# Mixture of experts in a gated block: the second bias as products of 12 rows, the residual put in first

## The chip, the cores and the metric

The kernel runs on one core of one Trainium2 chip. The metric is device time in microseconds (us) for one launch. TensorE (PE in the profile) multiplies matrices, VectorE (DVE) and GpSimd (POOL) do elementwise work, ScalarE (ACT) evaluates functions, SyncE (SP) only issues transfers here. Each engine runs its own instructions in order; semaphores order the engines among each other.

## The reference

Input `x` has 4 batches of 256 tokens with 256 features. The block adds a gated cross attention, then a gated transformer layer: `out = x1 + tanh(g_ffn) * ffn(x1)`. The layer is a layer norm, attention with 16 heads of 128, a residual, a second layer norm and a mixture of four experts. Only this last part is touched:

```
raw  = softmax(x @ w_gate)                      # [tokens, 4]
top_vals, top_idx = top_k(raw, 2)
comb = softmax(top_vals) scattered to [tokens, 4]
hmid = gelu(x @ we1[e] + be1[e])                # per expert e, 256 wide
eout = hmid @ we2[e] + be2[e]
moe  = sum over e of comb[:, e] * eout[:, e]
```

So the second bias contributes `comb @ be2`, a product over four experts. All is computed in f32 accuracy; products of f32 are made from a high part, rounded to the format that TensorE takes in one pass (F32R), and the low rest.

## The kernel before

The 1024 tokens stand as eight tiles of 128 partitions (`NT`), two per batch. `yacc` holds the running output of the second layer, `x_sb` the block's residual. Attention loops over eight pairs of heads with four batches each and takes most of the span; its last output projections end near 400 us, and then the experts follow. Tokens are handled in two halves `c` of 512, experts `e` in each: `m = 4c + e`, eight steps. Order on each engine is written out by hand.

**TensorE.** `middle(n)` makes 128 hidden features for 512 tokens (six products of 512 columns: high by low, low by high, high by high, two slices). There are 16, alternating between banks 0 and 1, and `middle(n)` waits until gelu `n - 2` has left its bank. `expert_out(m)` is 24 products of 256 columns into two banks (6 and 7, or 2 and 3), one for each batch `hf`; it waits for the low parts of the hidden features (`c_gL`) and from `m = 2` on for VectorE's accumulation of `m - 2`. The gate's logits are made transposed, in four strips of 32 partitions of bank 5, then turned by two transposes after `expert_out(0)`. After `expert_out(1)` come `middle(4)` to `middle(7)`, then an `expert_out` after every second `middle`.

**ScalarE** takes gelu out of the bank into `G` and writes its high part to `GH` (L834, L839). Ahead of gelu 4 it evaluates the two exponentials of the gates (L827, L829), each waiting for VectorE. Functions need a table; loading one is an instruction of its own.

**GpSimd** makes the low parts: `GL = G - GH` (L579), and for the normed hidden state (L575).

**VectorE** copies the logits from PSUM (L1190), waits for the turn, copies the gates (L1192), finds the softmax, the two largest and their weights (L1194 to L1227) in a `gate` tile of 128x32, and then does for each step `m`, with `yacc` as an input and an output:

```
ins = dve.scalar_tensor_tensor(yacc[:, n, :], be2_rows[:, e, :], gate[:, 4 * n + e:4 * n + e + 1], yacc[:, n, :], ...)   # L1240, bias
ins = dve.scalar_tensor_tensor(yacc[:, n, :], out_bank(m, hf)[:, 256 * t:256 * (t + 1)], gate[...], yacc[:, n, :], ...)  # L1249
```

four tiles each, so 32 of either kind. `be2_rows` is the bias spread over all 128 partitions by a single broadcast transfer (L318). After the last expert of a half, `yacc * tanh(g_ffn) + x_sb` follows for each batch (L1256, `small[:, 97]` is the gate of the block), and SP writes that batch out (L321). `link` on an engine makes the next instruction wait for the one before.

Of the kernel before, what the change touches and what calls it, by code (L numbers as in the profile page):

```python
# [8 lines left out]
F32R = mybir.dt.float32r  # L9
# [3 lines left out]
ALU = mybir.AluOpType  # L13
ACT = mybir.ActivationFunctionType
AX = mybir.AxisListType

P = 128
B, S, D = 4, 256, 256
# [12 lines left out]
NU = NP * U  # L31
LEAD = 6

E, I, IT = 4, 256, 2
NE = E * IT
# [13 lines left out]
def build_kernel(nc, x, ctx_in, cst, cols, rows, bv, wqkv, wo, w_out_t, w_gate, be2, we, out):  # L49
    with ExitStack() as stack:  # L50
# [10 lines left out]
        x_sb = sb("x_sb", [P, NT, D])  # L61
# [10 lines left out]
        yacc = sb("yacc", [P, NT, D])  # L72
# [4 lines left out]
        small = sb("small", [P, 160])  # L77

        stg = sb("stg", [P, 3, KT, 256])
# [5 lines left out]
        wvH = sb("wvH", [P, KT, 256], F32R)  # L85
        wvL = sb("wvL", [P, KT, 256], F32R)
# [35 lines left out]
        be2_rows = stg[:, 0:2, :, :].rearrange("p w k n -> p (w k n)").rearrange("p (e n) -> p e n", e=E)  # L122

        nh = sb("nh", [P, 2, D])
        qn = sb("qn", [P, 2, 2, D])
# [26 lines left out]
        bank = [ps(f"bank{n}") for n in range(8)]  # L152
# [5 lines left out]
        ident = cst_sb[:, C_ID:C_ID + P]  # L158
# [10 lines left out]
        c_nh c_tr c_hT c_hH c_h gate_zero d_be c_logit c_lgT c_lg_pe c_be c_mid c_gelu c_gH c_gL c_exp_pe c_acc c_fin"""  # L169
        s = {n: sem(n) for n in names.split()}  # L170

        def wait(eng, name, value):
# [100 lines left out]
        def _(sp):  # L273
# [44 lines left out]
            sp.dma_start(be2_rows, be2.rearrange("(o e) n -> o e n", o=1).to_broadcast([P, E, D])).then_inc(s["d_be"], 16)  # L318
            for b in range(B):
                sp.wait_ge(s["c_fin"], b + 1)  # L320
# [270 lines left out]
        def _(act):  # L591
# [103 lines left out]
            for p in range(NPX + VLAG):  # L695
                b, k = divmod(p, XP)
# [146 lines left out]
        def _(dve):  # L843
            seq = [0]

            def link(ins):

                seq[0] += 1
                ins.then_inc(s["dve_seq"], 1)
                dve.wait_ge(s["dve_seq"], seq[0])  # L850
# [65 lines left out]
            q = qn[:, 0, 0, 0:P].rearrange("p (h d) -> p h d", d=XD)  # L916
# [271 lines left out]
            V3 = lambda a: gate[:, a:a + 32].rearrange("p (t e) -> p t e", e=E)  # L1188
            dve.wait_ge(s["c_logit"], 1)
            dve.tensor_copy(nh[:, 0, :], bank[5][:, 0:256]).then_inc(s["c_lgT"], 1)  # L1190
            dve.wait_ge(s["c_lg_pe"], 1)
            link(dve.tensor_copy(Gt(0, 32).rearrange("p (b t e) -> p t b e", t=2, e=E),  # L1192
                                 bank[4][:, 0:256].rearrange("p (t b w) -> p t b w", t=2, b=B)[:, :, :, 0:E]))
# [34 lines left out]
            dve.wait_ge(s["d_be"], 16)  # L1228
            dve.wait_ge(s["b_yadd"], NU // 2)

            for m in range(2 * E):

                c, e = divmod(m, E)
                for hf in range(2):
                    b = 2 * c + hf
                    if m:
                        dve.wait_ge(s["c_acc"], 2 * (m - 1) + hf + 1)
                    for t in range(2):
                        n = 2 * b + t
                        ins = dve.scalar_tensor_tensor(yacc[:, n, :], be2_rows[:, e, :], gate[:, 4 * n + e:4 * n + e + 1], yacc[:, n, :],  # L1240
                                                       ALU.mult, ALU.add)
                    ins.then_inc(s["c_be"], 1)
                for hf in range(2):
                    b = 2 * c + hf
                    dve.wait_ge(s["c_exp_pe"], 2 * m + hf + 1)
                    dve.wait_ge(s["c_be"], 2 * m + hf + 1)
# [5 lines left out]
                    if e == E - 1:  # L1252
                        dve.wait_ge(s["c_acc"], 2 * m + hf + 1)
                        y = yacc[:, 2 * b:2 * b + 2, :].rearrange("p t n -> p (t n)")
                        xb = x_sb[:, 2 * b:2 * b + 2, :].rearrange("p t n -> p (t n)")
                        dve.scalar_tensor_tensor(y, y, small[:, 97:98], xb, ALU.mult, ALU.add).then_inc(s["c_fin"], 1)  # L1256


        @block.tensor
        def _(pe):  # L1260
# [291 lines left out]
            def middle(n):  # L1552
                if n >= 2:
                    pe.wait_ge(s["c_gelu"], n - 1)
                if n == NE:
                    pe.wait_ge(s["c_h"], B)
                middle_part(n, 0, 512).then_inc(s["c_mid"], 1)

            def expert_out(m):
# [4 lines left out]
                for hf in range(2):  # L1564
# [5 lines left out]
                                    [((GH[:, m % 2, k, cut], GL[:, m % 2, k, cut]), (we2H[:, 2 * e + k, :], we2L[:, 2 * e + k, :])) for k in range(IT)])  # L1570
                    ins.then_inc(s["c_exp_pe"], 1)

            pe.wait_ge(s["we_ready"], NP)
            for b in range(2):
                pe.wait_ge(s["c_h"], b + 1)
# [104 lines left out]
```

## Time and profile before

| | |
|---|---|
| time, three runs | 469.63 us median (467.46 to 471.44) |
| the profiled execution | 466.32 us, of it the span of instructions 464.2 |
| busy, share of the span | TensorE 411.2 us (89%), VectorE 370.1 (80%), GpSimd 297.6 (64%), ScalarE 286.5 (62%) |
| instructions | TensorE 3135 products, VectorE 1144, ScalarE 650, GpSimd 429 |
| granted TensorE clock, mean | 0.990 |

All stretches below are in us from the start of the span. A busy share is an average over stages with different limits; what a change in one stage is worth is read from that stage, by what ends its waits last. The chain of waits is followed back from the last instruction: at each step to what released it, or to the instruction before it on its engine. The clock is a share of full speed (2.4 GHz).

### The profile page before, as it was taken

Reading aid. Unit: us, or ns where it says so; the run is one execution under the profiler, and the core shown is the slowest. Engines: PE = TensorE matmul, PEld = TensorE weight load, DVE = VectorE, ACT = ScalarE, POOL = GpSimd, SP = SyncE. Lnnn points to the kernel's source line nnn. Section 1 sums busy time; section 2 is a strip of 40 time slices with the busy share of each in tenths; the row PEclk is TensorE's granted clock in tenths of the full one; section 3 lists DMA queues with packets and bytes.
Section 4 is the critical chain, followed back from the end, with each engine's and each line's share of the span. In section 5 each row is a group of like instructions: output and inputs, shape, how many; then the busy total and the mean of one; then the engine's idle time right before and its main releaser. Section 6 shows DMA issues by size and latency. Waiting matters only on the chain.

```text
span 464.2 us, 10317 instructions
## 1 busy us (share of the span) xinstructions
PE 411.2 (89%) x3135; PEld 357.7 (77%) x3150; DVE 370.1 (80%) x1144; ACT 286.5 (62%) x650; POOL 297.6 (64%) x429
## 2 busy tenths in 40 slices
PE   0477997998898899999999999999999995688994
PEld 0356876886786799899899898998998984577994
DVE  3855568677789988798788888898887868968997
ACT  3357674765235778677677677677677688174440
POOL 5898969720598597486687687677677534163551
PEclk9999999999999999999999999999999999979999
DMA  5600000200255885865865855975855654000011
GB/s 148 195 3 2 1 1 4 92 3 1 47 114 120 180 150 119 193 144 108 195 141 116 189 127 116 203 133 112 215 119 116 146 83 99 7 1 1 1 45 46
DMA packets 71795, 44.53 MB, mean 96 GB/s; under 512 B 57424, under 2 KB 60112, under 8 KB 71760
## 3 DMA queue, kind: packets, MB, share of 16 engines
q1 hardware_dynamic: 67680, 35.42, 36.0%
q10 hardware_dynamic: 4080, 8.69, 6.8%
q8 instruction: 17, 0.28, 0.2%
q14 instruction: 18, 0.15, 0.1%
HBM read 13.68 MB, written 1.05 MB: 32 GB/s over the span
## 4 chain that ended last, share of the span: by engine, by line
PE 67%; DVE 18%; issue 5%; ACT 3%; POOL 3%; DMA 2%; ACTq 0%; SPq 0%; DVEq 0%; POOLq 0%
PE bank L1395 35%; PE bank L1463 5%; PE bank L1510 5%; DVE yacc L1240 3%; PE bank L1462 3%; PE bank L1511 3%; DVE yacc L1249 2%; PE bank L1335 2%; PE bank L1376 2%; POOL room L511 2%; PE bank L1290 2%; PE bank L1311 2%; PE bank L1336 1%; PE bank L1357 1%; DMA qk_room<-qk_room 1%
## 5 line engine op out<-in xcount | busy, mean ns | idle before, releaser
L772 ACT ACTIVATE probs<-sm,nm 128x128 f32<-128x128 f32 (+1 forms) x128 | 57.2, 449 | 43.0 <-DVE nm L1126 43.0
L764 ACT ACTIVATE probs<-turned 128x768 uint16<-128x768 uint16 x64 | 69.1, 1080 | 19.3 <-DMA turned<-halves 18.0
L1395 PE MATMUL bank<-hH,qk_parts 128*128 128x512 f32 x240 | 75.4, 395 | 0.0
L524 POOL COPY halves<-probs 128x768 uint16<-128x768 uint16 x64 | 52.7, 824 | 35.0 <-DVE probs L1172 35.0
L511 POOL TENSOR_TENSOR room<-room,qk_room 128x512 f32<-128x512 f32 x32 | 41.2, 1289 | 33.7 <-DMA qk_room<-qk_room 28.7
L1395 PE MATMUL bank<-hL,qk_parts 128*128 128x512 f32 x120 | 57.7, 481 | 0.9 <-DVE room L1043 0.9
L1395 PEld LDWEIGHTS bank<-hH,qk_parts 128*128 128x128 f32 x240 | 45.2, 188 | 9.5
L1043 DVE SCALAR_TENSOR_TENSOR room<-bank,qk_bias,cst_sb 128x512 f32<-128x512 f32 x64 | 47.5, 742 | 0.0
L1395 PE MATMUL bank<-woL,o_parts 128*128 128x256 f32 x128 | 38.7, 302 | 9.8 <-DVE o_parts L1114 4.0
L1014 DVE TENSOR_REDUCE nxm<-bank 128x2 bf16<-128x512 f32 (+1 forms) x48 | 32.8, 688 | 18.0 <-PE bank L1336 17.4
L1395 PE MATMUL bank<-woH,o_parts 128*128 128x256 f32 x256 | 46.9, 281 | 0.0
L511 POOL TENSOR_TENSOR room<-room,q_room 128x512 f32<-128x512 f32 x32 | 41.2, 1289 | 6.2 <-DMA q_room<-q_room 6.1
L656 ACT ACTIVATE probs<-bank 128x512 f32<-128x512 f32 x48 | 28.4, 596 | 24.9 <-PE bank L1352 14.0
L781 ACT ACTIVATE o_parts<-bank,bv_pair 128x256 fp32r<-128x256 f32 x64 | 30.0, 468 | 16.9 <-PE bank L1511 10.2
L1395 PEld LDWEIGHTS bank<-woH,o_parts 128*128 128x128 f32 x256 | 39.4, 189 | 0.0
L1395 PE MATMUL bank<-wvL,hH 128*128 128x256 f32 x128 | 38.7, 302 | 0.7 <-ACT V L732 0.7
L1510 PE MATMUL bank<-probs,V 128*128 128x256 f32 x128 | 38.2, 379 | 0.2 <-ACT probs L764 0.2
L1463 PE MATMUL bank<-room 128*128 128x256 f32 x128 | 38.2, 380 | 0.0
L579 POOL TENSOR_TENSOR qk_parts<-G,o_parts 128x512 fp32r<-128x512 f32 x16 | 21.7, 1369 | 23.5 <-ACT o_parts L839 23.2
L1395 PE MATMUL bank<-wvH,hH 128*128 128x256 f32 x128 | 36.1, 282 | 0.0
L1395 PE MATMUL bank<-wvH,hL 128*128 128x256 f32 x128 | 36.0, 282 | 0.0
L1043 DVE SCALAR_TENSOR_TENSOR qk_room<-bank,qk_bias,cst_sb 128x512 f32<-128x512 f32 x32 | 24.0, 749 | 14.7 <-PE bank L1395 14.4
(233 smaller groups left out, 1269.0 us busy)
## 6 DMA issues: line engine op xcount, KB each, us to landing
qk_room<-qk_room SPq DMA_DIRECT2D x64, 128.0 KB, 2.4
q_room<-q_room SPq DMA_DIRECT2D x64, 128.0 KB, 2.4
stg<-in_wqkv ACTq DMA_DIRECT2D x6, 768.0 KB, 5.8
stge<-in_we ACTq DMA_DIRECT2D x7, 256.0 KB, 3.1
stg<-in_wqkv SPq DMA_DIRECT2D x2, 768.0 KB, 4.9
stgo<-in_wo ACTq DMA_DIRECT2D x6, 256.0 KB, 3.5
x_sb<-in_x SPq DMA_DIRECT2D x4, 256.0 KB, 4.2
turned<-halves SPq DMA_TRANSPOSE x64, 2.8
```

The lines of the kernel that those rows point to most:

```text
L511: pool.tensor_tensor(v, v, qk_sw[q], ALU.subtract).then_inc(s["rope_done"], 1)
L524: pool.tensor_copy(halves[:, j % 2, :, :], PR[:, j % 2, 0:384].bitcast(U16).rearrange("p (n h) -> p h n", h=2)).then_inc(s["b_split"], 1)
L579: pool.tensor_tensor(GL[:, (n // 2) % 2, n % 2, :], G[:, n % 2, :], GH[:, (n // 2) % 2, n % 2, :].bitcast(F32), ALU.subtract).then_inc(s[" ...
L656: act.activation(prob_slot(m, z), PT_B[p % 2][:, :], ACT.Exp).then_inc(s["s_exp"], 1)
L764: act.activation(PTs[:, 1 - q, 0:384].bitcast(U16).rearrange("p (n h) -> p h n", h=2), turned[:, (j - 3) % 4, :, :].rearrange("p (h c) n - ...
L772: ins = act.activation(PR[:, q, a:e], sm[:, q, a:e], ACT.Exp, bias=nm[:, q, t:t + 1], scale=-1.0, accum_out=rs[:, q, t:t + 1])
L781: act.activation(oH[:, ((j - 4) // 2) % 2, q, :], value_bank(j)[:, 0:256], ACT.Identity, bias=head_bias(j)).then_inc(s["b_oH"], 1)
L1014: dve.tensor_reduce(nxm[:, m % 3, a:a + len(heads)], S_B[p % 2][:, :].rearrange("p (h n) -> p h n", h=len(heads)), AX.X, ALU.max, negate=T ...
L1043: return dve.scalar_tensor_tensor(out.rearrange("p (b t) -> p b t", b=2), source[:, :].rearrange("p (b t) -> p b t", b=2), qk_bias[:, c:c ...
L1395: ins = pe.matmul(outp, l, r, start=(m == 0), stop=(m == n - 1))
L1463: pe.matmul(S_B[j % 2][:, P:3 * P], QT[:, 2 * r, second], QT[:, 2 * r + 1, both], start=True, stop=True).then_inc(s["b_s"], 1)
L1510: pe.matmul(value_bank(j)[:, 0:256], V[:, 2 * b, r * HD:(r + 1) * HD], PTs[:, q, 0:256], start=True, stop=False)
```

## The change

- The bias becomes a product on TensorE. `gates` is split in a high and a low part and packed on 12 columns of a strip of 32 (high, low, high), turned by two transposes (`pack_turn`) and copied to `gates_turned`; `be2_parts` holds, on the same 12 rows of each strip, the bias's high, high and low part. One product over 12 rows then gives `gates @ be2` to the precision of three products. `second_bias(c)` makes four such products of 256 columns for a half, into banks 4 and 5; VectorE adds them with two additions of 128x512.
- The 12 rows come by twelve transfers of 4 rows in place of the broadcast; VectorE splits them, between the copy of the logits and that of the gates.
- The residual is put in ahead: `yacc * tanh(g_ffn) + x_sb` is done before the experts (batches 0 and 1 ahead of the gates, 2 and 3 after expert 1), and the weights of the gates are multiplied by `tanh(g_ffn)`.
- The two-way softmax of the top values is `0.5 +- 0.5 tanh`, with ScalarE's Tanh moved from ahead of gelu 4 to ahead of gelu 5.

```diff
+            for q in range(4):
+                for r in range(3):
+                    row = 32 * q + E * r
+                    sp.dma_start(be2_raw[row:row + E, :], be2).then_inc(s["d_be"], 16)
...
                 if n == 4:
                     act.wait_ge(s["c_gmax"], 1)
                     act.activation(gate[:, 64:96], gate[:, 32:64], ACT.Exp).then_inc(s["c_gexp"], 1)
+                if n == 5:
                     act.wait_ge(s["c_gdiff"], 1)
-                    act.activation(gate[:, 400:408], gate[:, 392:400], ACT.Exp).then_inc(s["c_gexp"], 1)
+                    act.activation(gate[:, 400:408], gate[:, 392:400], ACT.Tanh, scale=-0.5).then_inc(s["c_gexp"], 1)
...
             dve.tensor_copy(nh[:, 0, :], bank[5][:, 0:256]).then_inc(s["c_lgT"], 1)
+            dve.wait_ge(s["d_be"], 16 * 12)
...
+            dve.tensor_scalar(half_g, small[:, 97:98], 0.5, None, ALU.mult)
+            dve.tensor_scalar(minus_half_g, small[:, 97:98], -0.5, None, ALU.mult)
+            dve.tensor_reduce(is_high, by_quad[:, :, 0:2 * E], AX.XY, ALU.add)
+            dve.tensor_reduce(is_low, by_quad[:, :, 2 * E:3 * E], AX.XY, ALU.add)
+            link(dve.tensor_copy(be2_high.bitcast(F32R), be2_raw))
+            link(dve.tensor_tensor(be2_low, be2_raw, be2_high, ALU.subtract))
+            link(dve.tensor_scalar(be2_low, be2_low, is_low, None, ALU.mult))
+            dve.scalar_tensor_tensor(be2_parts, be2_high, is_high, be2_low, ALU.mult, ALU.add).then_inc(s["c_half"], 1)
...
+            residual_form(0)
+            residual_form(1)
             dve.wait_ge(s["c_lg_pe"], 1)
...
-            link(dve.tensor_scalar(Gt(248, 8), Gt(400, 8), 1.0, None, ALU.add))
-            link(dve.reciprocal(Gt(256, 8), Gt(248, 8)))
-            link(dve.tensor_tensor(Gt(264, 8), Gt(256, 8), Gt(400, 8), ALU.mult))
+            dve.tensor_scalar(Gt(256, 8), Gt(400, 8), half_g, half_g, ALU.mult, ALU.add)
+            link(dve.tensor_scalar(Gt(264, 8), Gt(400, 8), minus_half_g, half_g, ALU.mult, ALU.add))
...
+            link(dve.tensor_copy(packed[:, :, :, 0:E].bitcast(F32R), gates))
+            dve.tensor_copy(packed[:, :, :, 2 * E:3 * E], packed[:, :, :, 0:E])
+            dve.tensor_tensor(packed[:, :, :, E:2 * E].bitcast(F32R), gates, packed[:, :, :, 0:E], ALU.subtract).then_inc(s["c_pack"], 1)
...
-                        ins = dve.scalar_tensor_tensor(yacc[:, n, :], be2_rows[:, e, :], gate[:, 4 * n + e:4 * n + e + 1], yacc[:, n, :],
-                                                       ALU.mult, ALU.add)
...
+            accumulate(0)
+            dve.wait_ge(s["c_pack_pe"], 1)
+            dve.tensor_copy(gates_turned, bank[4][:, 0:256]).then_inc(s["c_gT"], 1)
+            add_biases(0)
+            accumulate(1)
+            residual_form(2)
+            residual_form(3)
+            accumulate(2)
+            accumulate(3)
+            accumulate(4)
+            add_biases(1)
+            for m in range(5, 2 * E):
+                accumulate(m)
...
+            def second_bias(c):
...
+                for hf in range(2):
+                    rows_ = slice(32 * (2 * c + hf), 32 * (2 * c + hf) + 3 * E)
+                    for t in range(2):
+                        ins = pe.matmul(bank[4 + hf][:, 256 * t:256 * (t + 1)], gates_turned[rows_, t * P:(t + 1) * P], be2_parts[rows_, :],
+                                        start=True, stop=True)
...
             middle(5)
+            pack_turn()
             middle(6)
-            for n in range(7, 2 * NE):
+            middle(7)
+            second_bias(0)
+            expert_out(2)
+            for n in range(8, 2 * NE):
                 middle(n)
+                if n == 11:
+                    second_bias(1)
                 if n % 2:
                     expert_out((n - 3) // 2)
```

`pack_turn` waits for `c_pack` and makes the two transposes into bank 4. `accumulate(m)` is the four accumulations of L1249; `add_biases(c)` waits for `second_bias(c)` and adds banks 4 and 5 to `yacc`; `accumulate(1)` and `accumulate(5)` wait for it.

## Rows read from the trace of the kernel before

**Rows 1.** Busy by stretch: from:to, us; PE, PEld, DVE, ACT, POOL; clock, DMA, GB/s.

```profile
424.45:425.81 1.36, 0.00 (x1) 0.00 (x1) 1.29 (x6) 1.32 (x3) 0.00 (x0) 1.00 0.00 0
425.81:457.83 32.02, 31.73 (x204) 28.27 (x204) 31.95 (x60) 14.98 (x23) 16.59 (x12) 1.00 0.05 17
```

**Rows 2.** End of the chain of waits: start, us, what.

```profile
460.90 0.75 DVE yacc L1256
```

**Rows 3.** TensorE in order of time: start, us, engine, line, operation [idle before, releaser].

```profile
425.81 0.51 PE L1395 MATMUL bank<-hL,weH 128*128 128x512 f32 x1 [1.36 <-ACT G L834]
...
429.12 0.39 PE L1395 MATMUL bank<-weL,o_parts 128*128 128x256 f32 x1 [0.24 <-POOL qk_parts L579]
...
432.05 0.39 PE L1395 MATMUL bank<-hL,weH 128*128 128x512 f32 x1
...
457.55 0.28 PE L1395 MATMUL bank<-weH,o_parts 128*128 128x256 f32 x1
```

**Rows 4.** VectorE on `yacc`, experts: count; ns min/median/max, first and last start.

```profile
L1240 DVE SCALAR_TENSOR_TENSOR yacc<-stg,gate,yacc x32: 470/474/1522, 425.0 to 458.0; 128x256 f32<-128x256 f32 x32
L1249 DVE SCALAR_TENSOR_TENSOR yacc<-bank,gate,yacc x32: 469/473/480, 426.6 to 460.4; 128x256 f32<-128x256 f32 x32
L1256 DVE SCALAR_TENSOR_TENSOR yacc<-yacc,small,x_sb x4: 752/819/1765, 440.8 to 460.9; 128x512 f32<-128x512 f32 x4
```

**Rows 5.** VectorE and GpSimd side by side; last row: ns min/median/max in attention.

```profile
429.27 3.34 DVE L1240 SCALAR_TENSOR_TENSOR yacc<-stg,gate,yacc 128x256 f32<-128x256 f32 x3
...
429.35 2.98 POOL L579 TENSOR_TENSOR qk_parts<-G,o_parts 128x512 fp32r<-128x512 f32 x2 [0.28 <-ACT o_parts L839]
...
L1171 DVE TENSOR_SCALAR probs<-probs,rs x64: 285/287/1437, 136.4 to 389.0; 128x128 f32<-128x128 f32 x64
```

**Rows 6.** VectorE and GpSimd around the logit copy, in order of time.

```profile
415.31 2.55 POOL L579 TENSOR_TENSOR qk_parts<-G,o_parts 128x512 fp32r<-128x512 f32 x2
417.81 1.29 POOL L575 TENSOR_TENSOR hL<-qk_room,hH 128x512 fp32r<-128x512 f32 x1
...
415.65 0.42 DVE L1190 COPY nh<-bank 128x256 f32<-128x256 f32 x1 [1.43 <-PE bank L1589]
418.86 0.19 DVE L1192 COPY gate<-bank 128x32 f32<-128x32 f32 x1 [2.79 <-PE bank L1595]
```

**Rows 7.** ScalarE at the gates, in order of time.

```profile
416.51 1.28 ACT L827 ACT_TABLE_LOAD   x1
419.53 0.23 ACT L827 ACTIVATE gate<-gate 128x32 f32<-128x32 f32 x1 [1.73 <-DVE gate L1195]
...
425.07 0.69 ACT L834 ACTIVATE G<-bank,cols_sb 128x512 f32<-128x512 f32 x1
425.79 0.63 ACT L839 ACTIVATE o_parts<-G 128x512 fp32r<-128x512 f32 x1
```

**Rows 8.** VectorE's gate arithmetic, two of its steps.

```profile
422.70 0.19 DVE L1216 TENSOR_TENSOR gate<-gate 128x32 f32<-128x32 f32 x1
...
423.34 0.17 DVE L1220 TENSOR_TENSOR gate<-gate 128x8 f32<-128x8 f32 x1
```

**Rows 9.** Turn of the gates, return from 32-column products, issue of the bias transfer.

```profile
L1595 PE MATMUL bank<-cst_sb,nh x2: 270/270/271, 418.4 to 418.6; 128*128 128x128 f32 x2
...
415.51 0.19 PEld L1395 LDWEIGHTS bank<-weL,o_parts 128*128 128x128 f32 x1 [0.41 <-issue]
...
391.74 0.53 SPq L318 DMA_DIRECT2D stg<-in_be  x1
```

**Rows 10.** ScalarE's Tanh at the front.

```profile
18.84 0.20 ACT L694 ACTIVATE small<-rows_sb 128x2 f32<-128x2 f32 x1 [0.26 <-DMA rows_sb<-in_rows]
```

**Rows 11.** Busy time by stretch around the clock's fall; columns as in Rows 1.

```profile
392.96:395.49 2.53, 0.00 (x2) 0.03 (x1) 2.46 (x9) 1.37 (x2) 0.00 (x0) 1.00 0.60 198
400.64:403.35 2.71, 0.00 (x1) 0.01 (x1) 2.57 (x9) 0.00 (x0) 1.18 (x1) 1.00 0.00 0
...
404.03:410.86 6.83, 5.64 (x26) 5.05 (x26) 6.33 (x27) 2.61 (x4) 1.27 (x1) 0.50 0.00 0
```

More of the change, by code:

```diff
@@ L121, in build_kernel @@
         gate = sb("gate", [P, 512])
-        be2_rows = stg[:, 0:2, :, :].rearrange("p w k n -> p (w k n)").rearrange("p (e n) -> p e n", e=E)
+        be2_raw, be2_high, be2_low, be2_parts = stg[:, 0, 0, :], stg[:, 0, 1, :], stg[:, 1, 0, :], wvH[:, 0, :]
+        gates_turned = wvL[:, 0, :]
         nh = sb("nh", [P, 2, D])
@@ L168, in build_kernel @@
         b_s b_max b_exp b_norm b_split d_pt0 d_pt1 b_merge b_pv b_oH b_oL b_wo b_yadd v_pe v_ready
-        c_nh c_tr c_hT c_hH c_h gate_zero d_be c_logit c_lgT c_lg_pe c_be c_mid c_gelu c_gH c_gL c_exp_pe c_acc c_fin"""
+        c_nh c_tr c_hT c_hH c_h gate_zero d_be c_logit c_lgT c_lg_pe c_half c_pack c_pack_pe c_gT c_be c_badd c_res c_mid c_gelu c_gH c_gL c_exp_pe c_acc"""
         s = {n: sem(n) for n in names.split()}
@@ L1190, in _, with residual_form @@
             dve.tensor_copy(nh[:, 0, :], bank[5][:, 0:256]).then_inc(s["c_lgT"], 1)
+            dve.wait_ge(s["d_be"], 16 * 12)
+            is_low, is_high = small[:, 142:143], small[:, 143:144]
+            by_quad = ident.rearrange("p (q w) -> p q w", q=4)
+            half_g, minus_half_g = small[:, 140:141], small[:, 141:142]
+            dve.tensor_scalar(half_g, small[:, 97:98], 0.5, None, ALU.mult)
[6 more added lines that the diff above has]
+            dve.scalar_tensor_tensor(be2_parts, be2_high, is_high, be2_low, ALU.mult, ALU.add).then_inc(s["c_half"], 1)
+            def residual_form(b):
+                y = yacc[:, 2 * b:2 * b + 2, :].rearrange("p t n -> p (t n)")
+                xb = x_sb[:, 2 * b:2 * b + 2, :].rearrange("p t n -> p (t n)")
+                dve.scalar_tensor_tensor(y, y, small[:, 97:98], xb, ALU.mult, ALU.add).then_inc(s["c_res"], 1)
+            dve.wait_ge(s["b_yadd"], NU // 2)
+            residual_form(0)
+            residual_form(1)
             dve.wait_ge(s["c_lg_pe"], 1)
@@ L1227, in _, with accumulate @@
             link(dve.tensor_tensor(Gt(0, 32), Gt(120, 32), Gt(152, 32), ALU.add))
-            dve.wait_ge(s["d_be"], 16)
-            dve.wait_ge(s["b_yadd"], NU // 2)
-            for m in range(2 * E):
+            packed = nh[:, 1, :].rearrange("p (t b w) -> p b t w", t=2, w=32)
+            gates = gate[:, 0:32].rearrange("p (b t e) -> p b t e", b=B, e=E)
+            link(dve.tensor_copy(packed[:, :, :, 0:E].bitcast(F32R), gates))
+            dve.tensor_copy(packed[:, :, :, 2 * E:3 * E], packed[:, :, :, 0:E])
+            dve.tensor_tensor(packed[:, :, :, E:2 * E].bitcast(F32R), gates, packed[:, :, :, 0:E], ALU.subtract).then_inc(s["c_pack"], 1)
+            def accumulate(m):
                 c, e = divmod(m, E)
@@ L1235, in _ @@
                     b = 2 * c + hf
-                    if m:
-                        dve.wait_ge(s["c_acc"], 2 * (m - 1) + hf + 1)
-                    for t in range(2):
-                        n = 2 * b + t
-                        ins = dve.scalar_tensor_tensor(yacc[:, n, :], be2_rows[:, e, :], gate[:, 4 * n + e:4 * n + e + 1], yacc[:, n, :],
-                                                       ALU.mult, ALU.add)
[L1242 to L1246, printed above, removed]
+                    dve.wait_ge(s["c_exp_pe"], 2 * m + hf + 1)
+                    if e == 0:
+                        dve.wait_ge(s["c_res"], b + 1)
+                    elif e == 1:
+                        dve.wait_ge(s["c_badd"], b + 1)
+                    else:
+                        dve.wait_ge(s["c_acc"], 2 * (m - 1) + hf + 1)
                     for t in range(2):
@@ L1251, in _, with add_biases @@
                     ins.then_inc(s["c_acc"], 1)
[L1252 to L1256, printed above, removed]
+            def add_biases(c):
+                dve.wait_ge(s["c_be"], c + 1)
+                for hf in range(2):
+                    b = 2 * c + hf
+                    dve.wait_ge(s["c_acc"], 2 * E * c + hf + 1)
+                    y = yacc[:, 2 * b:2 * b + 2, :].rearrange("p t n -> p (t n)")
+                    dve.tensor_tensor(y, y, bank[4 + hf][:, :], ALU.add).then_inc(s["c_badd"], 1)
+            accumulate(0)
[11 more added lines that the diff above has]
+                accumulate(m)
         @block.tensor
@@ L1571, in expert_out, with pack_turn @@
                     ins.then_inc(s["c_exp_pe"], 1)
+            def pack_turn():
+                pe.wait_ge(s["c_pack"], 1)
+                for t in range(2):
+                    ins = pe.transpose(bank[4][:, t * P:(t + 1) * P], nh[:, 1, t * P:(t + 1) * P], ident)
+                ins.then_inc(s["c_pack_pe"], 1)
+            def second_bias(c):
+                if c == 0:
+                    pe.wait_ge(s["c_gT"], 1)
+                    pe.wait_ge(s["c_half"], 1)
+                else:
+                    pe.wait_ge(s["c_badd"], 2)
+                for hf in range(2):
+                    rows_ = slice(32 * (2 * c + hf), 32 * (2 * c + hf) + 3 * E)
+                    for t in range(2):
+                        ins = pe.matmul(bank[4 + hf][:, 256 * t:256 * (t + 1)], gates_turned[rows_, t * P:(t + 1) * P], be2_parts[rows_, :],
+                                        start=True, stop=True)
+                ins.then_inc(s["c_be"], 1)
             pe.wait_ge(s["we_ready"], NP)
```

3 lines of the change are left out of this document (1 added, 2 removed).

## The prediction, made before the changed kernel ran

> **What bounds the kernel now.** Everything that the change touches lies in the last 50 us, the experts, so the first view to read is busy time by stretch: from 425.81 to 457.83 TensorE is busy 31.73 of 32.02 us and VectorE 31.95 [rows 1]. Two engines look full, and only the order of events tells which one the other waits for. The chain of waits ends in VectorE's residual sum at 460.90 + 0.75 = 461.65 [rows 2], and from 425 on it names almost nothing but the accumulations, which would make VectorE the bound. TensorE's own order of time says otherwise: after the products that start at 425.81 it stands still once for 0.24 us before 429.12, and its last product starts at 457.55 and lasts 0.28, to 457.83 [rows 3]. It never waits for an accumulation. VectorE keeps up and is late only at the end, by 461.65 - 457.83 = 3.82 us. Removing VectorE work can give back that tail and no more, unless TensorE starts its dense stretch earlier. Where that stretch starts is set by one stall: 1.36 us before 425.81, for the first gelu after the gate's exponentials.
>
> The 32 bias additions take 0.47 us each, up to 1.52 [rows 4]. That is at least 15 us of VectorE time removed, of which I count at most 3.8 on the end.
>
> **What the change adds ahead of the gates.** Before, VectorE idles 2.79 us between the logit copy (415.65 + 0.42 = 416.07) and 418.86, while TensorE finishes expert 0 [rows 6]. The change fills this gap with two one-element scalings and two small sums (about 0.4 us together, at some 0.1 to 0.2 each as in the gate arithmetic [rows 8]), a copy of 128x256, a subtraction, a scaling, a fused multiply-add, and two residual sums of 128x512. Alone they cost, with the 0.47 of an addition for a 256-wide pass and 0.75 for a 512-wide one [rows 4], 0.4 + 4 x 0.4 + 2 x 0.7 = 3.4 us: 0.6 more than the gap. But they don't run alone: GpSimd runs three subtractions from 415.31 to 419.10 [rows 6]. What that does is seen later in the same trace: three bias additions beside two GpSimd subtractions took 3.34 us instead of 1.4, while the two took 2.98 [rows 5]; the longest addition took 1.52. With two SBUF inputs VectorE waits for the end of the GpSimd instruction, then goes, and they alternate. Scalings that read and write SBUF are held too: one of 128x128 had 287 ns as its median and 1437 at most [rows 5]. Accumulations from PSUM are not: 469 to 480 ns over all 32 [rows 4]. So the copy goes in behind the first subtraction (416.6), the subtraction of the low part behind the second (delayed by the copy to 418.05; done 418.3, as the held ones end some 0.3 after the holder), the scaling behind the third (419.5, done 419.7), the multiply-add at 420.2, the two residual sums at 421.5. The gate arithmetic starts at 421.46 in place of 418.86: **+2.6 us**, bounded by +0.6 (no hold) and +2.9.
>
> **What happens in the gates.** ScalarE's exponential moves from 419.53 [rows 7] to 422.1. Its return to gelu now comes before the second transcendental: load 1.28, gelu 0.69, copy 0.63 [rows 7] after 422.36 give 425.05, and GpSimd then subtracts the low part for 1.3 us, to 426.4. Before, GpSimd was idle during the gates; now that subtraction meets the gate arithmetic, which by +2.6 stands then near what was 422.70 [rows 8], a product of two SBUF inputs. It waits until 426.4, and the rest up to the gate difference (423.34 + 0.17 before, 0.8 us on [rows 8]) ends at 427.2: another **+1.0** (0 to 1.3). The tanh ends at 427.46. Behind it stand two scalings, three products or sums, and three packing instructions at 0.1 to 0.2 each with four waits for the one before: 1.4 us, to 428.85. Only then can TensorE turn the packed gates.
>
> On ScalarE every tanh before ran among exponentials with the one table of the front (18.84) [rows 10]. The Trainium skill ("ScalarE: Activation LUTs", Table sets) lists tanh beside exp and beside sigmoid, and not in gelu's set; by that list two more loads come in, and no row here shows tanh beside gelu. Two loads of 1.28 [rows 7] would cost nothing here: the exponential's own load started at 416.51, 3.0 ahead of it and of the wait in front of it [rows 7], so the first fits between 425.05 and 427.2, and the return to gelu (to 428.75, gelu 429.4) is over before TensorE has done the one middle product that precedes its use. I count 0, and up to 1.28 if the load stands behind the wait.
>
> **What it adds on TensorE.** Where before 425.81 waits for gelu, the new order waits for the pack. Two turns of 0.27 [rows 9], 0.25 together as they overlap, let the middle products start at 429.1: **+3.3 us**, and TensorE is idle from 424.45 to 428.85, 4.4 us instead of 1.36 [rows 1]. The 0.24 us stall before 429.12 goes (-0.24), since GpSimd is done by then. Eight products of 12 rows by 256 columns: the 24 of expert 2 stand from 429.12 to 432.05, 0.12 each [rows 3]; I take the same, 0.49 for four, **+0.98** in all; nothing hides them, as TensorE is full. The nearest row for a change of the array's shape is the return from the 32-column gate products, 0.41 us idle [rows 9]; four such changes bound the eight products at 0.98 + 1.64 = 2.6, and 0.4 is the lower end, if products of different rows run together. I take the low value, since that 0.41 also holds the end of the products before. The Trainium skill ("TensorEngine Tiling (Array Packing)", Key Properties) says that changing the tiling mode drains TensorE; by it the sum is nearer to 2.6. The copy of the turned gates (0.42 like the one at 415.65 [rows 6]) stands behind the first four accumulations and is done near 430.3, before the first bias products (432.0): hidden. The bias additions and the other two residual sums, about 4 x 0.7, fall to a VectorE that has lost 15 us: hidden. Expert 3 waits for accumulation 1, which by this comes near 435 against 437: hidden by 2 us.
>
> On SP one broadcast issue of 0.53 at 391.74 [rows 9] becomes twelve: about 6.4 us, so the last is issued near 398; VectorE asks at 416, and nothing else is queued on SP until the first output. Cost 0.
>
> **The tail.** TensorE ends at 457.83 + 3.3 - 0.24 + 0.98 = 461.9. VectorE then owes one half of the last expert, two accumulations, 0.9 us, in place of 3.82: 462.8 against 461.65. Output and what follows are the same: **+1.1 us**.
>
> **The clock.** This idle stretch is the longest that TensorE has in the kernel. After 2.71 us idle (400.64 to 403.35) the granted clock fell from 1.00 to 0.50 at 404.03 and stayed there for 6.83 us, with TensorE busy 5.64 of them; after 2.53 us idle (392.96 to 395.49) it did not fall [rows 11]. With 4.4 us idle I expect a fall. At 0.50, which is 1.2 of 2.4 GHz, half of the 5.64 busy us is lost, **+2.8** (0 if it doesn't fall, 3.4 if it holds a full stretch of dense products).
>
> **Sum:** 1.1 + 2.8 = +3.9 us. The profiled execution took 466.32, with a span of 464.2; the sum gives 470.2. The median of the three runs lies 3.3 above it, so on that scale the forecast is 469.6 + 3.9 = 473.5, 0.8% slower: within 1%, about what a measurement of this kernel can tell from no change.
>
> **Rivals.**
> - *Late pack, clock holds.* As above without the fall: 469.6 + 1.1 = 470.7. For it: 2.53 us idle was survived and 1.36 too. Against it: this one is 1.7 longer than the one that wasn't. Chance 0.2.
> - *The gap holds the preparation.* The holds by GpSimd don't reach the new instructions, the gates start 0.6 late and the pack is ready at 425.9, as gelu was. TensorE then restarts about 0.4 later than before, plus 0.98 - 0.24, and ends at 459.0; with 0.9 behind it VectorE ends at 459.9: -1.8, 467.8. For it: the small gate instructions show no hold. Against it: no GpSimd instruction ran beside them, and [rows 5] show the holds. Chance 0.14.
> - *Table load on the path, slower.* Tanh is not in gelu's set and its load is issued after the wait for the gate difference, at 427.2. Place: between the difference and the pack; price 1.28; it decides as soon as ScalarE's load starts later than 425.9. It adds to the forecast: 473.5 + 1.3 = 474.8, 1.1% slower. For it: the list quoted above. Against it: the load at 416.51 ran ahead of its wait. Chance 0.08.
> - *The additions were the bound after all*, as the chain's names suggest: 15 us less, 455. Against it: TensorE's 31.73 of 32.02 busy without one wait for them. Chance 0.02.
>
> The forecast itself has 0.56.
>
> **How the numbers follow.** Range 467.0 to 475.5: its low end takes in the case without holds and 0.8 us of scatter (the runs shown lie from 467.46 to 471.44), its high end the load on the path; beyond it lie a fall that holds longer and drains of 1.6. Slower by over 1% (474.3) needs the table load, a drain or a full 3.4 at 0.50: 0.25. Faster by over 1% (464.9) needs more than the tail can give: 0.07. Within: 0.68.
>
> **What would show it.** Step by step, in the changed profile: GpSimd-held copy and subtraction of 1 us and more after 416, the gate arithmetic starting near 421.5, VectorE idle between its accumulations, TensorE idle some 4 us after 424.45 with the wait put down to the pack, a granted clock of 0.50 behind it, products of 12 rows at 0.12 each, 0.9 us between TensorE's end and VectorE's. The prediction is wrong if TensorE resumes near 426, if the clock stays at 1.00, or if TensorE waits again between 432 and the end.

## The result, and the profile after

In 20 runs of either kernel the changed one took 470.81 us (median; 469.27 to 475.67) and the kernel before 467.67 (465.65 to 471.68). The ratio is 1.0069, with a 95% interval from 1.0047 to 1.0092: about 3.2 us slower, 0.7%.

| profiled execution | before | after |
|---|---|---|
| span, mean granted clock | 464.2, 0.990 | 470.2, 0.978 |
| TensorE busy, products | 411.2, 3135 | 417.2, 3145 |
| VectorE busy, instructions | 370.1, 1144 | 357.9, 1127 |
| end of the logit copy | 416.08 | 418.56 |
| from there to the end of VectorE | 45.58 | 49.09 |

The two spans differ by 6.0 us, but 2.5 of it lie ahead of the logit copy. So everything below is counted from the end of that copy to the end of VectorE, which is the stretch that the change rewrites; there the changed kernel is 3.51 us longer.

Busy time by stretch comes first, with the columns of [rows 1]: two stretches ahead of the experts, then TensorE's wait, the 0.50 clock behind it, and the rest.

```profile
155.90:159.30 3.40, 3.40 (x15) 3.40 (x16) 3.27 (x10) 2.90 (x8) 2.11 (x3) 0.50 0.94 165
388.00:391.40 3.40, 2.93 (x11) 2.27 (x9) 2.84 (x11) 2.85 (x9) 0.47 (x1) 0.50 0.32 60
426.93:432.25 5.32, 0.00 (x1) 0.01 (x1) 4.76 (x17) 1.70 (x4) 2.54 (x2) 0.69 0.00 0
432.25:435.76 3.51, 3.51 (x10) 2.83 (x11) 1.84 (x5) 0.23 (x1) 0.00 (x0) 0.50 0.00 0
435.76:466.73 30.97, 30.97 (x206) 27.37 (x204) 14.82 (x32) 12.99 (x20) 12.94 (x10) 1.00 0.05 18
```

The third line answers to the first of [rows 1]: TensorE idles 5.32 us where it idled 1.36, and behind it the clock stands at 0.50, the lower of its two levels, for 3.51 us of work. In the last line TensorE is full (30.97 of 30.97) and VectorE no longer is (14.82; it had 31.95 of 32.02 in [rows 1]). The first two lines are the first two of four stretches at 0.50 ahead of the logit copy, some 3.4 us each; at these two places the kernel before ran at 1.00, and it had a single stretch at 0.50 between its first 30 us and the logit copy, of 6.83 us [rows 11]. They stand in the 2.5 us upstream; what each of them cost was not measured.

TensorE in order of time, to be set against [rows 3]:

```profile
432.25 0.69 PE L1619 MATMUL bank<-cst_sb,nh 128*128 128x128 f32 x2 [5.32 <-DVE nh L1257]
432.58 0.78 PE L1437 MATMUL bank<-hL,weH 128*128 128x512 f32 x1
...
436.68 0.39 PE L1437 MATMUL bank<-hH,weH 128*128 128x512 f32 x1
436.99 0.50 PE L1632 MATMUL bank<-wvH,wvL 12*128 12x256 f32 x4
437.43 0.39 PE L1437 MATMUL bank<-weL,o_parts 128*128 128x256 f32 x1
437.65 0.28 PE L1437 MATMUL bank<-weH,qk_parts 128*128 128x256 f32 x1
...
466.45 0.28 PE L1437 MATMUL bank<-weH,o_parts 128*128 128x256 f32 x1
```

The 5.32 us are put down to VectorE's `nh`, the packed gates, as the prediction had it. The dense products start at 432.58, 14.02 us after the logit copy; before they started 9.73 after it. The products of 12 rows stand at 436.99, and the last product ends at 466.73.

VectorE in order of time, then GpSimd, answering to [rows 6, 8]:

```profile
418.77 1.30 DVE L1204 CAST stg<-stg 128x256 fp32r<-128x256 f32 x1
420.10 1.40 DVE L1205 TENSOR_TENSOR stg<-stg 128x256 f32<-128x256 f32 x1
421.54 0.35 DVE L1206 TENSOR_SCALAR stg<-stg,small 128x256 f32<-128x256 f32 x1
...
423.65 0.18 DVE L1218 COPY gate<-bank 128x32 f32<-128x32 f32 x1
...
427.49 1.14 DVE L1242 TENSOR_TENSOR gate<-gate 128x32 f32<-128x32 f32 x1
...
430.81 1.29 DVE L1256 COPY nh<-nh 128x32 f32<-128x32 f32 x1
```

```profile
417.35 2.56 POOL L583 TENSOR_TENSOR qk_parts<-G,o_parts 128x512 fp32r<-128x512 f32 x2
419.83 1.38 POOL L579 TENSOR_TENSOR hL<-qk_room,hH 128x512 fp32r<-128x512 f32 x1
427.30 1.28 POOL L583 TENSOR_TENSOR qk_parts<-G,o_parts 128x512 fp32r<-128x512 f32 x1 [6.08 <-ACT o_parts L843]
430.80 1.26 POOL L583 TENSOR_TENSOR qk_parts<-G,o_parts 128x512 fp32r<-128x512 f32 x1 [2.22 <-ACT o_parts L843]
```

Read the two side by side. The copy (1.30) ends 0.16 behind GpSimd's 419.91, the subtraction (1.40) 0.29 behind 421.21, and the scaling, with GpSimd at rest, takes 0.35. At 427.49 a product of 128x32 takes 1.14 instead of 0.19 beside the low part of gelu 4, and at 430.81 a copy of the pack takes 1.29 beside the low part of gelu 5.

ScalarE in order of time, answering to [rows 7]:

```profile
424.57 1.28 ACT L838 ACT_TABLE_LOAD   x1
425.86 0.69 ACT L838 ACTIVATE G<-bank,cols_sb 128x512 f32<-128x512 f32 x1
...
429.27 0.21 ACT L833 ACTIVATE gate<-gate 128x8 f32<-128x8 f32 x1 [2.06 <-DVE gate L1246]
429.39 0.67 ACT L838 ACTIVATE G<-bank,cols_sb 128x512 f32<-128x512 f32 x1
```

After the one load at 424.57 come gelu, tanh and gelu again with no load between them.

VectorE on `yacc` by operation and form, with the columns of [rows 4], and the end of the chain, answering to [rows 2]:

```profile
L1273 DVE SCALAR_TENSOR_TENSOR yacc<-bank,gate,yacc x32: 472/478/485, 432.1 to 467.2; 128x256 f32<-128x256 f32 x32
L1212 DVE SCALAR_TENSOR_TENSOR yacc<-yacc,small,x_sb x4: 744/745/748, 422.3 to 441.0; 128x512 f32<-128x512 f32 x4
L1284 DVE TENSOR_TENSOR yacc<-yacc,bank x4: 678/682/690, 437.5 to 453.8; 128x512 f32<-128x512 f32 x4
```

```profile
449.36 17.38 PE bank L1437 x120
...
466.77 0.48 DVE yacc L1273
```

Of 32 + 32 narrow instructions 32 are left, and four wide additions have come; the residual's four take 744 to 748 ns, where one took 1765 in [rows 4]. The chain now names TensorE's products up to the last accumulations: VectorE ends at 467.65, 0.92 behind TensorE, where it ended 3.82 behind before.

### The profile page after: what moved, and what is told of

Read it like the earlier page. It is cut to its first block, busy times and chain, and to the rows that moved or that the text cites. A ratio compares the mean times of both kernels' runs of the same rounds, so it can differ in the third digit from the quotient of the medians.

```text
span 470.2 us, 10333 instructions
## 1 busy us (share of the span) xinstructions
PE 417.2 (89%) x3145; PEld 362.4 (77%) x3160; DVE 357.9 (76%) x1127; ACT 286.4 (61%) x650; POOL 296.9 (63%) x429
## 4 chain that ended last, share of the span: by engine, by line
PE 74%; DVE 13%; issue 4%; ACT 3%; POOL 3%; DMA 2%; ACTq 0%; SPq 0%; DVEq 0%; POOLq 0%
PE bank L1437 41%; PE bank L1552 5%; PE bank L1505 5%; PE bank L1504 3%; PE bank L1553 3%; PE bank L1377 2%; PE bank L1418 2%; POOL room L515 2%; PE bank L1332 2%; PE bank L1353 2%; PE bank L1378 1%; DMA qk_room<-qk_room 1%; PE bank L1399 1%; PE bank L1403 1%; PE bank L1392 1%
## 5 line engine op out<-in xcount | busy, mean ns | idle before, releaser
L1437 PE MATMUL bank<-woH,o_parts 128*128 128x256 f32 x256 | 48.3, 287 | 0.0
L1437 PEld LDWEIGHTS bank<-woH,o_parts 128*128 128x128 f32 x256 | 40.5, 194 | 0.0
L583 POOL TENSOR_TENSOR qk_parts<-G,o_parts 128x512 fp32r<-128x512 f32 x16 | 20.7, 1302 | 30.7 <-ACT o_parts L843 30.3
L1552 PE MATMUL bank<-probs,V 128*128 128x256 f32 x128 | 39.6, 391 | 0.4 <-ACT probs L768 0.4
```

What stands on the lines that cost most here:

```text
L583: pool.tensor_tensor(GL[:, (n // 2) % 2, n % 2, :], G[:, n % 2, :], GH[:, (n // 2) % 2, n % 2, :].bitcast(F32), ALU.subtract).then_inc(s[" ...
L1437: ins = pe.matmul(outp, l, r, start=(m == 0), stop=(m == n - 1))
L1552: pe.matmul(value_bank(j)[:, 0:256], V[:, 2 * b, r * HD:(r + 1) * HD], PTs[:, q, 0:256], start=True, stop=False)
```

## The experiments

Each experiment is read in two ways: the time, as a ratio to the kernel before with its 95% interval, and, in one profile, the stretch from the end of the logit copy to the end of VectorE. Against the kernel before the two agree within 0.8 us in every run here. The intervals are some 0.3% (1.4 us) to either side, so where two orders differ by less than about 2 us the profile carries the reading and not the time.

**No additions.** The kernel before without the 32 bias additions (the second bias is left out of the result); nothing else moves.

```
 for t in range(2):
     n = 2 * b + t
-    ins = dve.scalar_tensor_tensor(yacc[:, n, :], be2_rows[:, e, :], gate[...], yacc[:, n, :], ALU.mult, ALU.add)
```

> The kernel before, with its 32 bias additions left out (the second bias is not applied). TensorE bounds the experts (theory): only VectorE's tail behind TensorE's end shrinks, from 3.82 us to some 1.7 (two accumulations and the residual sum), so 2 to 3 us less than before, about 465. Rival, the additions are the bound: 13 to 15 us less, about 453.

Measured: ratio to before 0.9942 [0.9908, 0.9976]; VectorE ends 43.57 us after the logit copy, 2.0 less than before. Its order of time on TensorE and VectorE:

```profile
427.92 0.50 PE L1387 MATMUL bank<-hL,weH 128*128 128x512 f32 x1 [1.36 <-ACT G L834]
...
459.61 0.28 PE L1387 MATMUL bank<-weH,o_parts 128*128 128x256 f32 x1
...
461.00 0.75 DVE L1248 SCALAR_TENSOR_TENSOR yacc<-yacc,small,x_sb 128x512 f32<-128x512 f32 x1
```

TensorE waits the same 1.36 us for the same gelu, and ends at 459.89, 41.70 after the logit copy, where it ended 41.75 after it before. Fifteen microseconds of VectorE work gave back part of the tail (1.86 is left of 3.82) and nothing else: the additions were not the bound. This kernel has the old broadcast transfer and its logit copy ended at 418.19, so a copy as late as that comes without the twelve transfers too.

**Pack late.** All parts of the change, with the turn of the gates and the bias products moved behind other TensorE work:

```
 middle(5)
-pack_turn()
 middle(6); middle(7)
-second_bias(0)
 expert_out(2)
+pack_turn()
 for n in range(8, 2 * NE):
     middle(n)
+    if n == 9: second_bias(0)
```

On VectorE `accumulate(1)` goes ahead of the copy of the turned gates, and `add_biases(0)` behind `accumulate(2)`.

> The changed kernel in another order: the packed gates are turned after expert 2's products and the bias products follow middle 9, so that TensorE does not stand before the pack. Theory (TensorE's wait for the pack, 5.3 us in the profile of the changed kernel, and the clock's fall behind it are the loss): expert 2 starts some 4 us earlier, 0.6 of it given back where the first bias products stand now; the time comes out some 3.5 to 4 us below the changed kernel, 0.5 to 1 us below the kernel before, with no 0.50 stretch right behind 430. Rival (the added products or the earlier stages are the loss): 3 us above the kernel before, as the changed kernel.

Measured: 1.0023 [0.9992, 1.0054]; 46.00 us after the logit copy, 3.1 less than the changed kernel and 0.4 more than before. I had expected it 0.5 to 1 us below before, with no stretch at 0.50; both were wrong, the time by 1 to 2 us. TensorE in order of time, and the stretch of the clock:

```profile
427.64 0.52 PE L1437 MATMUL bank<-hL,weH 128*128 128x512 f32 x1 [1.81 <-ACT G L838]
...
430.67 0.55 PE L1437 MATMUL bank<-weL,o_parts 128*128 128x256 f32 x1 [0.39 <-DVE yacc L1273]
```

```profile
427.96:431.36 3.40, 3.02 (x9) 2.03 (x8) 3.33 (x9) 2.50 (x5) 2.56 (x2) 0.50 0.00 0
```

The wait for the pack is gone. What is late next is gelu 5 (1.81 us) and, 3 us on, an accumulation (0.39), and the clock fell to 0.50 for 3.40 us although the idle time was a third of the changed kernel's. So most of what the changed kernel loses hangs on where the pack stands. The gates still start 5.1 us after the logit copy here, and that this is what makes gelu 5 late is argued, not shown by this run alone (in "order", below, the gates start at 2.79 and no wait for a gelu is left).

**Gap empty.** The four splitting instructions of the bias and the first two residual sums are left out, and with them the second bias's rows and the residual of batches 0 and 1 from the result; the products and additions still run:

```
-link(dve.tensor_copy(be2_high.bitcast(F32R), be2_raw))
-link(dve.tensor_tensor(be2_low, be2_raw, be2_high, ALU.subtract))
-link(dve.tensor_scalar(be2_low, be2_low, is_low, None, ALU.mult))
-dve.scalar_tensor_tensor(be2_parts, ...).then_inc(s["c_half"], 1)
+dve.memset(small[:, 150:151], 0.0).then_inc(s["c_half"], 1)
...
-residual_form(0); residual_form(1)
+dve.memset(...)   # two, one element each, signal c_res
```

> The changed kernel without the four passes that split the bias and without the first two residual sums (both left out, nothing in their place). Theory: the gate arithmetic starts 2.3 us earlier behind the copy of the logits (2.8 us as before, not 5.1), the pack is ready 2 to 2.5 us earlier, TensorE's wait is about 3 us and not 5.3; time 0.7 us above the kernel before if the clock still falls, 0.8 below if it doesn't. Rival (ScalarE's order, with gelu 4 ahead of the tanh, makes the pack late, not the work in the gap): pack and time as in the changed kernel, 3 us above.

Measured: 1.0058 [1.0029, 1.0086]; 48.30 us after the logit copy, 0.8 less than the changed kernel.

```profile
419.92 0.19 DVE L1215 COPY gate<-bank 128x32 f32<-128x32 f32 x1 [2.47 <-PE bank L1655]
...
429.19 0.69 PE L1616 MATMUL bank<-cst_sb,nh 128*128 128x128 f32 x2 [3.68 <-DVE nh L1254]
```

```profile
427.70:434.50 6.80, 5.31 (x14) 4.12 (x14) 3.23 (x11) 1.32 (x2) 1.13 (x2) 0.50 0.00 0
```

The gates start 2.79 us after the logit copy (417.13), as before, and the pack is ready 1.6 earlier than in the changed kernel (I had expected 2 to 2.5). TensorE idles 3.68 instead of 5.32. But the clock's fall, once there, now covers 5.31 busy us instead of 3.51, which takes back about half of the gain. I had expected 0.7 us above before if the clock fell, and it came out 2.7 above: the tanh, ready at 424.56, now waits for gelu 4 and starts at 425.41, and two of the weights' small instructions are held beside the low parts of gelu 4 and 5 (1.24 us for a scaling of 128x8, 1.18 for a product of 128x32). So the pack gained less than the gates did, and the clock cost more; the rival, ScalarE's order, has a part in it. By time this kernel can't be told from the changed one (their intervals overlap). Emptying the gap alone mends little.

**Kept busy.** The changed kernel with 40 products ahead of the turn of the gates, which no one reads:

```
 middle(5)
+pe.wait_ge(s["c_lgT"], 1)
+for r in range(40):
+    pe.matmul(bank[5][:, 0:256], we2H[:, 0, 0:P], we2H[:, 1, :], start=True, stop=True)
 pack_turn()
```

> The changed kernel with 40 products of 128x256 that nothing reads (4.7 us at 0.12 each), put where TensorE waits for the pack. The pack is as late as before. Theory: the granted clock stays at 1.00 behind the pack, and the time is 1.5 us below the changed kernel by the 0.50 stretch that its profile shows (up to 2.8), so 0.3 to 1.6 us above the kernel before. Rival (the fall costs nothing, the wait alone counts): 3 us above the kernel before.

The wait in the first line is for the logit copy, which is over by then. Measured: 1.0042 [1.0013, 1.0072], an interval that overlaps the changed kernel's; 47.58 us after the logit copy, 1.51 less than the changed kernel, as expected. TensorE in order of time and busy by stretch:

```profile
432.46 0.44 PE L1619 MATMUL bank<-cst_sb,nh 128*128 128x128 f32 x2 [0.58 <-DVE nh L1257]
432.65 0.48 PE L1437 MATMUL bank<-hL,weH 128*128 128x512 f32 x1
...
436.06 0.39 PE L1437 MATMUL bank<-weL,o_parts 128*128 128x256 f32 x1
```

```profile
427.07:431.88 4.81, 4.81 (x41) 4.61 (x39) 4.25 (x15) 1.72 (x4) 2.20 (x2) 1.00 0.00 0
432.46:437.00 4.54, 4.54 (x26) 3.58 (x27) 2.66 (x7) 2.56 (x4) 1.23 (x1) 1.00 0.00 0
```

The pack comes as late as in the changed kernel (13.7 us after the logit copy), and the clock stays at 1.00. From the turn to the first product of expert 2 it takes 436.06 - 432.46 = 3.60 us, and the changed kernel takes 437.43 - 432.25 = 5.18 for the same instructions: the fall cost 1.58.

**Tanh first.** The changed kernel with ScalarE's Tanh back ahead of gelu 4:

```
-                if n == 5:
-                    act.wait_ge(s["c_gdiff"], 1)
+                    act.wait_ge(s["c_gdiff"], 1)
```

> The changed kernel with the tanh back ahead of gelu 4, nothing else. Theory (GpSimd's low parts of gelu 4 and 5 hold gate and pack instructions, 1.0 and 1.1 us in the profile of the changed kernel): with GpSimd idle during the gates no instruction of the gate arithmetic or of the pack takes over 0.3 us, the pack is ready some 11.3 us behind the copy of the logits in place of 13.6; TensorE then waits for gelu 4, to 12.0 in place of 14.0; time some 2 us below the changed kernel, 1 above the kernel before. Rival (they are slow for another reason, and gelu 4 early is worth what it was meant to be): the same two instructions take over 1 us, time as the changed kernel or later.

Measured: 1.0025 [0.9998, 1.0053]; 47.18 us after the logit copy, 1.9 less than the changed kernel, as expected. VectorE and TensorE in order of time, then the stretch of the clock:

```profile
428.22 0.19 DVE L1241 TENSOR_TENSOR gate<-gate 128x32 f32<-128x32 f32 x1
...
430.59 0.18 DVE L1255 COPY nh<-nh 128x32 f32<-128x32 f32 x1
...
430.92 0.44 PE L1618 MATMUL bank<-cst_sb,nh 128*128 128x128 f32 x2 [3.21 <-DVE nh L1256]
```

```profile
432.37:435.78 3.41, 3.41 (x9) 2.27 (x7) 0.40 (x2) 2.09 (x4) 3.09 (x3) 0.50 0.00 0
```

GpSimd's low part of gelu 4 now starts only at 432.01, behind the pack, so neither the product (0.19) nor the copy (0.18) is held, and TensorE idles 3.21. The turn starts 11.6 us after the logit copy (419.32) in place of 13.7. The clock falls here too, with TensorE at work through all of the 3.41 us, about as much as in the changed kernel (3.51), so the fall hardly bears on the difference of 1.9.

**Order.** All parts of the change, with the TensorE order of "pack late", and on VectorE the split of the bias behind `accumulate(1)` and the packing behind `accumulate(0)`; in the gap stay the scalings and the two residual sums.

```
 accumulate(0)
+(the three instructions that pack the gates)
 accumulate(1)
+dve.wait_ge(s["d_be"], 16 * 12)
+(the two sums and the four instructions that split be2)
 dve.wait_ge(s["c_pack_pe"], 1)
```

> All parts of the change in another order: only the two scalings and the residual sums stand in the gap, the split of the bias and the pack behind the first accumulations, the turn of the packed gates behind expert 2, the first bias products behind middle 9. Theory: the gate arithmetic starts some 3.1 us behind the copy of the logits, TensorE goes on after middle 5 with less than 0.5 us idle, the clock holds, and the tail stays at 0.9 us: from the copy of the logits to VectorE's end 42 us in place of 45.6 before and 49.1 after, so 3.5 us below the kernel before (0.992). Rival (the bias products and turns cost TensorE more than their 1.2 us, or the accumulations stall it): as the kernel before, or above.

Measured: 0.9984 [0.9954, 1.0014], no difference that can be told; 44.71 us after the logit copy, against 45.58 before and some 42 expected. VectorE, GpSimd and TensorE in order of time:

```profile
424.60 1.27 DVE L1239 TENSOR_SCALAR gate<-gate,small 128x8 f32<-128x8 f32 x1 [0.74 <-ACT gate L833]
...
426.10 1.19 DVE L1241 TENSOR_TENSOR gate<-gate 128x32 f32<-128x32 f32 x1
...
427.43 1.25 DVE L1243 TENSOR_TENSOR gate<-gate 128x32 f32<-128x32 f32 x1
...
424.54 5.49 POOL L583 TENSOR_TENSOR qk_parts<-G,o_parts 128x512 fp32r<-128x512 f32 x4 [4.75 <-ACT o_parts L843]
...
429.74 0.36 PE L1436 MATMUL bank<-weL,o_parts 128*128 128x256 f32 x1 [2.47 <-DVE yacc L1258]
```

A new wait took the gain: three of the weights' small instructions stand beside the low parts of gelu 4, 5 and 6 and are held 1.2 us each, the accumulations start late, and TensorE waits 2.47 for one of them. So the rival came out: the accumulations stall TensorE. The clock held its 1.00 through that.

**Order, tanh first.** The same, with Tanh ahead of gelu 4 as above.

> The reordered kernel with the tanh ahead of gelu 4. Theory (in the reordered kernel GpSimd's low parts of gelu 4, 5 and 6 hold three of the four instructions that make the weights, 1.2 us each, and TensorE waits 2.5 us for the first accumulation): no such hold, TensorE waits instead some 1.6 us for gelu 4 behind the table load, as before the change; from the copy of the logits to VectorE's end 43.8 us in place of 44.7, about 1.5 to 2 us below the kernel before. Rival (order of ScalarE does not matter there): as the reordered kernel.

Measured: 0.9967 [0.9935, 0.9998]; 44.51 us after the logit copy (expected 43.8). Against "order" (0.9984, 44.71) this is no difference that can be told, so by time the rival came out, though the waits changed:

```profile
426.56 0.50 PE L1435 MATMUL bank<-hL,weH 128*128 128x512 f32 x1 [1.70 <-ACT G L837]
```

The five weights' instructions take 0.18 to 0.29 us and are no longer held, but gelu 4 now stands behind the exponential and the tanh, and TensorE waits 1.70 for it.

**Low part waits.** "Order", with GpSimd's low part of gelu 5 told to wait until the gates' weights are summed:

```
+dve.tensor_tensor(Gt(0, 32), Gt(120, 32), Gt(152, 32), ALU.add).then_inc(s["c_gates"], 1)
...
 pool.wait_ge(s["c_gH"], n + 1)
+if n == 5:
+    pool.wait_ge(s["c_gates"], 1)
```

> The reordered kernel in which GpSimd starts the low part of gelu 5 only when the weights are made (tanh ahead of gelu 5 as in the change). Theory: one instruction held in place of three, weights ready some 2 us earlier, TensorE waits under 1 us before expert 2's products (for that low part, or for the first accumulation); from the copy of the logits to VectorE's end 43.1 us, about 2.5 us below the kernel before (0.995). Rival (TensorE's wait has another cause): 44.7 us, as the reordered kernel.

Measured: 0.9959 [0.9931, 0.9988], medians 465.89 us against 468.66; 43.09 us after the logit copy, as expected (43.1).

```profile
424.68 1.27 DVE L1241 TENSOR_SCALAR gate<-gate,small 128x8 f32<-128x8 f32 x1 [0.83 <-ACT gate L835]
...
426.18 0.19 DVE L1243 TENSOR_TENSOR gate<-gate 128x32 f32<-128x32 f32 x1
...
428.18 0.39 PE L1439 MATMUL bank<-weL,o_parts 128*128 128x256 f32 x1 [0.82 <-POOL qk_parts L585]
```

Of the weights' instructions one is still held and the next are not, and TensorE waits 0.82 in place of 2.47. This version is faster than both kernels, if by little: its interval ends at 0.9988 (the changed kernel stands at 1.0069), and on the stretch it is 2.49 us below before and 6.0 below the changed one, with every part of the change in it.

## Why the prediction was right, point by point

The sign and the size came out as forecast: +3.9 us forecast, 3.2 [2.2, 4.3] measured (the interval of the ratio times 467.67). In absolute time 473.5 was 2.7 too high, of which 2.0 is the median of the kernel before: 469.63 in the three runs shown, 467.67 in twenty. The mechanism was read rightly: TensorE is the bound, the additions are worth only VectorE's tail, the pack comes late, and the clock falls behind the wait. None of the prediction's three signs of being wrong came: TensorE did not resume early, the clock did not stay at 1.00, and TensorE did not wait again up to its end. But two terms were mis-sized by about 1 us each, in opposite directions: the late pack by too little and the clock by too much. That the sum came so near is in part luck; with either term alone put right it would have been 4.8 or 2.7.

| term, us | predicted | measured |
|---|---|---|
| dense products start later | +3.3 | +4.15 |
| stall for the low part | -0.24 | -0.50 |
| products of 12 rows | +0.98 | +1.24 |
| clock | +2.8 | +1.58 |
| tail of VectorE | -2.92 | -2.90 |
| sum | +3.9 | +3.57 (3.51 by the trace) |

- *Start of the dense products.* 14.02 - 9.73 = 4.29 us, of which 0.14 belong to the turns at 0.50 (0.33 from turn to first product, 0.19 in "kept busy"). The gates started 5.09 after the logit copy in place of 2.79: +2.30 for a predicted 2.6; the copy and the subtraction were held, the scaling was not, as GpSimd had finished. (In "pack late" the subtraction and the scaling were held, 1.41 and 1.27, the copy was not, 0.40, and the gates started 5.1 after the copy all the same.) The collision with the low part of gelu 4 was 0.95 for a predicted 1.0. What failed is the step "three packing instructions at 0.1 to 0.2 each": the copy among them met the low part of gelu 5 and took 1.29, **+1.1** that I had not counted. I had asked what GpSimd does beside the weights, and not what it does 3 us later. "Tanh first", where neither of the two is held, shows their price together: the turn starts 2.1 us earlier, of which 1.9 are left at the end.
- *Clock.* It fell, as forecast, but the step "with TensorE busy 5.64 of them" took the size from the wrong place. The 0.50 lasted 6.8 us again (428.94 to 435.76), and it began while TensorE still stood idle: only 3.51 of it were work. "Kept busy" gives the price: 1.58. (The idle stretch was not the longest of the kernel, as I wrote, but the longest behind its start, where TensorE waits once for 15.7 us in the kernel before; nothing in the sum rests on this.) "Gap empty" shows the other side: with the wait shortened, 5.31 of the 6.80 were work.
- *Products of 12 rows.* From 436.68 to 437.43 are 0.75 where middle products follow each other at 0.235, and the first product behind takes 0.22 (437.43 to 437.65) in place of 0.12: 0.62 for the four, 1.24 for both halves. That is nearer to my low value than to the bound of 2.6. The Trainium skill ("TensorEngine Tiling (Array Packing)", Key Properties) has TensorE drain when the tiling mode changes, by which the sum would be nearer to 2.6. The trace is in keeping with a drain but not with that price: 0.62 is 0.14 more than four products at 0.12, and no run here shows what makes up the 0.14.
- *Stall.* It stood in the trace as 0.24 us idle, but from start to start it had cost 0.64 - 0.235 + 0.10 = 0.50, so more was saved.
- *Tables.* Cost nothing, as counted. The Trainium skill ("ScalarE: Activation LUTs", Table sets) does not list tanh with gelu; the trace differs, with gelu, tanh and gelu behind a single load, and the measurement decides. The rival with the load on the path is out.
- *Transfers.* Twelve issues on SP took 0.26 to 0.47 each, 4.2 us in all (6.4 predicted), done by 397.3. Nobody waited for them: "pack late" has them all and its logit copy ended at 416.05.
- *Tail.* 0.92 for 0.9; "no additions" shows apart from all else that the 15 us of VectorE work were worth 2 us.

So each part works as it was meant to, and the gain was there: TensorE's 1.24 us of new products is less than the 2.9 of the tail. It went into one new wait, the pack ahead of middle 6, and into the clock behind that wait. With both taken away by order and one wait of GpSimd's, the same parts are 2.5 us faster than before on the stretch.

What stays open: why the clock fell upstream at other places in the profile of the changed kernel (the 2.5 us ahead of the logit copy). Logit copies ended between 416.05 and 419.33 in all kernels here. Where the clock stood at 0.50 in a single stretch between the first 30 us and this copy (before, "pack late" and the three orders) it ended by 416.5, where there were two to four such stretches from 417.1 on; the late ones are in kernels with and without the twelve transfers. It is not needed for the 3.2 us, which the stretch behind the copy accounts for by itself.

## What to carry to other kernels

An engine that looks full may owe its partner only a tail: look at whether the other engine ever waits for it before counting its work as time. Work that is cheap in instructions is dear when a full engine's queue stands behind its last step, so put the consumer of a long chain of small steps as late in the queue as its result allows. Where VectorE works beside GpSimd, follow GpSimd's schedule over the whole chain and let GpSimd wait at the one place where a held instruction is on the path.

## What the runs showed of the hardware

- A hold by GpSimd is as long for a tiny instruction as for a big one: scalings of 128x8 (1.27; 0.29 when not held) and copies of 128x32 (1.29; 0.18) that read and write SBUF were held about as long as a subtraction of 128x256 (1.40). The 32 accumulations that read PSUM were not (472 to 485 ns).
- The length of the idle time alone does not tell whether the clock falls: it fell behind 1.81 us in "pack late", and not behind 2.47 in "order" nor behind the 2.53 of [rows 11]. The runs don't show what else decides it.
- The 0.50 can begin while TensorE is still idle, and what it costs is the part of it in which TensorE works: 1.58 us here, with 3.51 of 6.8 us at work.
